# Delta attention: Gram matrices at the end of the projections, a sigmoid in quarters, state scalings moved, two heads ahead of the first spreading

## The reference

```python
q = silu(dwconv(x @ Wq)); k = silu(dwconv(x @ Wk)); v = silu(dwconv(x @ Wv))
a = sigmoid(x @ Wa + ba); beta = sigmoid(x @ Wb + bb)
for t in range(T):                       # per batch and head, S is 128 x 128
    err = S @ (k_t * D**-0.5) - v_t
    S = a_t * S - (beta_t * err) outer (k_t * D**-0.5)
    o_t = S @ q_t
out = (layernorm(o) * ln_g + ln_b) * sigmoid(x @ Wg) @ Wo
```

## Time and profile before

| what | value |
|---|---|
| median of 3 runs | 2659.15 us (2654.32 to 2659.25) |
| the profiled execution | 2658.91 us |
| its span | 2657.0 us |
| PE busy | 2083.4 us, 78% |
| DVE, ACT, POOL busy | 1521.6 (57%), 1182.6 (45%), 1037.5 (39%) |

### The profile page before, as it was taken

The page is one execution under the profiler, slowest core; times in us unless marked ns, Lnnn a source line. Parts: engine busy times, 40 slices in busy tenths (PEclk is TensorE's granted clock), DMA queues, the critical chain, the costliest instruction groups (busy, mean ns, idle before and its releaser), DMA issues. The chain is left out here.

```text
span 2657.0 us, 45220 instructions
## 1 busy us (share of the span) xinstructions
PE 2083.4 (78%) x16876; PEld 1611.6 (61%) x16888; DVE 1521.6 (57%) x3266; ACT 1182.6 (45%) x2893; POOL 1037.5 (39%) x965
## 2 busy tenths in 40 slices
PE   8497438978897987857798577977779676768798
PEld 5365225646565865746587466866668665546586
DVE  2222642237574344687676876767868678246532
ACT  3212411126364334754465545655456454326433
POOL 0222122210003552586335862467724757100254
PEclk9698769989998997958798687986689777889899
DMA  8422012110004212321222212322122222020430
GB/s 281 134 24 53 3 43 67 23 44 2 23 2 134 102 18 75 97 69 49 84 90 68 89 45 83 93 69 69 57 88 80 66 69 78 19 58 2 118 118 16
DMA packets 138317, 179.47 MB, mean 68 GB/s; under 512 B 62048, under 2 KB 114544, under 8 KB 132992
## 3 DMA queue, kind: packets, MB, share of 16 engines
q1 hardware_dynamic: 129952, 166.46, 20.5%
q0 software_dynamic: 8160, 10.26, 2.5%
HBM read 154.52 MB, written 22.17 MB: 66 GB/s over the span
## 5 line engine op out<-in xcount | busy, mean ns | idle before, releaser
L2672 DVE SCALAR_TENSOR_TENSOR XT<-M_delta,CW_delta,XT 128x256 f32<-128x256 f32 x576 | 250.0, 495 | 82.7 <-ACT M_delta L2463 52.6
L2146 PE MATMUL PS<-XP_delta,X 128*128 128x268 f32 (+1 forms) x1024 | 244.0, 391 | 15.5 <-DMA X<-in_L_attn_b_heads 15.5
L2146 PEld LDWEIGHTS PS<-XP_delta,X 128*128 128x128 f32 x1024 | 194.8, 191 | 68.2 <-DMA X<-in_L_attn_b_heads 19.3
L1541 PE MATMUL PS<-XP_rffn,UW_rffn 128*128 128x512 f32 x816 | 195.3, 396 | 5.1 <-POOL UW_rffn L1495 4.6
L1541 PEld LDWEIGHTS PS<-XP_rffn,UW_rffn 128*128 128x128 f32 x816 | 156.4, 192 | 38.9 <-issue 6.0
L1273 ACT ACTIVATE PR_attn<-PS,NM_attn 128x256 f32<-128x256 f32 (+1 forms) x384 | 131.0, 449 | 102.5 <-DVE NM_attn L1343 102.5
L1495 POOL TENSOR_TENSOR UW_rffn<-W_rffn,UW_rffn 128x512 fp32r<-128x512 f32 x34 | 43.7, 1286 | 298.8 <-ACT UW_rffn L1602 298.8
L561 POOL DMA_INDIRECT sums<-XS_moe,token_moe x46 | 71.7, 1559 | 220.8 <-ACT XS_moe L661 196.9
L2590 ACT ACTIVATE S_delta<-S_delta,AO_delta 128x128 f32<-128x128 f32 x512 | 156.9, 396 | 0.0
L1663 DVE TENSOR_TENSOR SU_rffn<-PS,CB_rffn 128x512 f32<-128x512 f32 x68 | 47.0, 692 | 179.7 <-PE PS L1541 157.3
L1504 POOL TENSOR_TENSOR HP_rffn<-HF_rffn,HP_rffn 128x512 fp32r<-128x512 f32 x68 | 92.5, 1380 | 116.3 <-ACT HP_rffn L1625 116.3
(11 more groups left out here) (459 smaller groups left out, 5271.4 us busy)
## 6 DMA issues: line engine op xcount, KB each, us to landing
M_delta<-gram_delta SPq DMA_DIRECT2D x32, 1280.0 KB, 5.9
X<-in_L_attn_b_heads SPq DMA_DIRECT2D x64, 512.0 KB, 3.5
EW<-in_L_ffn_w SPq DMA_DIRECT2D x24, 512.0 KB, 9.1
CB_rffn<-routes_rffn SPq DMA_DIRECT2D x20, 512.0 KB, 21.9
XN<-in_L_attn_b_outs SPq DMA_DIRECT2D x16, 512.0 KB, 3.6
F_delta<-in_L_attn_b_outs SPq DMA_DIRECT2D x4, 2048.0 KB, 9.5
W_rffn<-in_L_ffn_tiles SPq DMA_DIRECT2D x4, 1536.0 KB, 12.5
slots<-pad SPq DMA_DIRECT2D x2, 2967.0 KB, 14.3
```

The costliest lines, as they stand in the source:

```text
L1541: last = nc.tensor.matmul(PS[:, 4 + 2 * n + q, :], UW[qw][:, r, (q * KD + k) * P:(q * KD + k + 1) * P], XP[qx][:, k, n * NB:(n + 1) * NB], ...
L2146: last = nc.tensor.matmul(PS[:, 1 + i, 0:B * (WIN - halo)], WH[:, r, i, k, :], XP[:, k, :, n * BT + halo:n * BT + WIN], start=(k == 0), st ...
L2672: nc.vector.scalar_tensor_tensor(TMP[:, r, i], RAW[:, r, i, :, tau:tau + BT], CW[:, i, h, tau:tau + 1], TMP[:, r, i], ALU.mult, ALU.add).t ...
```

## The change

- Both halves' Gram matrices are made before the states phase, heads 0 to 13 first, then heads 14 and 15, which alone wait for the last silus and keys. `gram(1)` no longer follows the states. The order of DVE's four `gram_rows` and SP's count (3 instead of 2) follow this.
- The sigmoid over A is split into four of 1024 columns, one behind each of ACT's first four groups in the states phase of the first half; the fourth releases POOL.
- `cuts` go from 14, 14, 20, 16 scalings in chunks 0 to 3 to 18, 18, 24, 4. Those of chunk 3 stand before the key rows instead of between them.
- In a block after the first, PE's list has `head(n, 0)` before `spread(n - 1, 0)` and `head(n, 1)` right after `centre(n - 1, 1)`, ahead of the first two projects; ACT's list has `evacuate(n, 0)` before `square(n - 1, 1)`.

```diff
-                sp.wait_ge(gr_d, z["gr_d"] + 2)
+                sp.wait_ge(gr_d, z["gr_d"] + 3)
                 scatter(0, 0)
...
-            def gram(o):
-
-                for h in range(H):
+            def gram(o, first, last_h):
+
+                for h in range(first, last_h):
...
                     variance(n - 1, 0)
+                if n < NBLK:
+                    head(n, 0)
+                if n:
                     spread(n - 1, 0)
-                for k in range(1, H // 2 + 1):
+                    centre(n - 1, 1)
+                if n < NBLK:
+                    head(n, 1)
+                if n:
+                    variance(n - 1, 1)
+                    project(n - 1, 0)
+                    project(n - 1, 1)
+                    spread(n - 1, 1)
+                for k in range(2, H // 2 + 1):
...
                 pe.wait_ge(ev_d, z["ev_d"] + 3 * H)
-                pe.wait_ge(act_d, z["act_d"] + 3 * H)
                 pe.wait_ge(raw_d, z["raw_d"] + H)
-                pe.wait_ge(k_d, z["k_d"] + H)
-                gram(0)
+                for first, last in ((0, H - 2), (H - 2, H)):
+                    pe.wait_ge(act_d, z["act_d"] + 3 * last)
+                    pe.wait_ge(k_d, z["k_d"] + last)
+                    for o in range(NO):
+                        gram(o, first, last)
...
-                gram(1)
                 for o in range(NO):
                     key_products(n, o)
...
-                for k in range(1, H // 2 + 1):
+                if n < NBLK:
+                    evacuate(n, 0)
+                if n:
+                    square(n - 1, 1)
+                if n < NBLK:
+                    evacuate(n, 1)
+                    silus(n, 0)
+                for k in range(2, H // 2 + 1):
...
+                    if not o and g < 4:
+                        part = AF[:, g * BH * BT // 4:(g + 1) * BH * BT // 4]
+                        last = nc.scalar.activation(part, part, ACT.Sigmoid)
+                        if g == 3:
+                            last.then_inc(a_d, 1)
...
-            cuts = [0, 14, 28, 48, BH]
+            cuts = [0, 18, 36, 60, BH]
...
-                nc.scalar.activation(AF, AF, ACT.Sigmoid).then_inc(a_d, 1)
                 states(n, 0)
...
+                        if jj == NI - 1:
+                            decay_state(lane, last)
                         for r in rows[:2]:
                             key_rows(n, o, r)
...
-                        else:
+                        elif jj + 1 < NI:
                             decay_state(lane, last)
-                            if jj + 1 < NI:
-                                answer(n, ci)
+                            answer(n, ci)
...
-                dve.wait_ge(gr_mm, n * 4 + 2 * o + i + 1)
+                dve.wait_ge(gr_mm, n * 4 + 2 * i + o + 1)
...
-                gram_rows(n, 0, 0)
-                gram_rows(n, 0, 1)
+                for i in range(2):
+                    gram_rows(n, 0, i)
+                    gram_rows(n, 1, i)
                 for g in range(1, NS, 2):
                     state_copy(n, 0, g)
-                gram_rows(n, 1, 0)
-                gram_rows(n, 1, 1)
```

More of the change, by code:

```diff
@@ L2505, in heads_and_norm @@
                         evacuate(n, 2 * k - 2)
-                        if k > 1:
-                            silus(n, 2 * k - 3)
+                        silus(n, 2 * k - 3)
                         evacuate(n, 2 * k - 1)
```

## The result

The changed kernel takes 2634.41 us (median of 6 runs, 2631.31 to 2640.3) against 2659.13 for the kernel before in the same session (6 runs, 2654.32 to 2660.09): ratio 0.9912, 95% interval 0.9899 to 0.9925. The forecast was 2625, with a range of 2613 to 2639. So the kernel is 24.7 us faster where 34.2 were worked out.

A forecast was written before the change was run, and what follows sets the result against it. Waits at engine handovers (projections' end, last chunk, block border) were taken to bound the delta stage, PE the heads stage; 18.7 + 11.6 + 3.9 = 34.2 us off 2658.9 gave 2625 us, range 2613 to 2639.

The forecast's parts named there:

- Scalings moved, 18.7 forecast: Last chunk of each block: PE's turn of W starts 4.66 us sooner, four times, 18.7 us saved.
- the cap of 21.1: Last chunk: the turn cannot pay more than DVE's 5.27 us wait per block, 21.1 us in all.
- The cost in chunks 0 to 2: Four more scalings in each chunk add 1.2 us, taken to lie in ACT's idle time: no cost.
- a bound of 4.8: Second half's first chunk, scalings ahead of `answer`: lost cover costs at most 1.2 us a block, 4.8 in all.
- Gram matrices and quarters, 11.6 forecast: End of projections to DVE's `base`: 3.1 us sooner in three blocks, 2.3 in block 0, 11.6 in all.
- the row was right: Table load before the sigmoid: 1.30 us by the profile row, against the skill's 2.66 with drain.
- The rival of an ACT that falls behind in the quarters: States phase: ACT later by 1.28 us a block, 5.1 in all, paid through POOL; 2630 us, chance 0.05.
- Two heads ahead, 3.9 forecast: Three block borders: PE resumes 1.3 us sooner at each, 3.9 us saved, between -3 and 9.2.
- the cold stretch: Border: PE's first 3.5 us at clock 0.50 may stay the same (gain 1.3) or vanish (1.75 us more).
- half clock (28 ns passes): Rival: Gram passes before the states take 6.4 us, costing 2.9 us in three blocks; 2633 us, chance 0.12.
- no gain at the border: Rival: swapped heads give nothing, 2629 us, or 2632 with 1 us of new stall each; chance 0.07.

The follow-up runs named there:

- Experiments 4 and 8: 4: changed kernel with the old cuts in first halves only, 2624.08 us. 8: changed kernel with the last errors copied ahead of the scalings, 2623.59 us.
- experiment 7: Changed kernel with 32 instead of 16 idle PE transposes at the end of each first half; one execution, 2635.96 us.
- experiment 5: Changed kernel with the sigmoid whole again ahead of the states, Gram matrices staying at the end of the projections; 2639.97 us, ratio 0.992.
- experiment 10: Changed kernel with the last errors copied early, the sigmoid whole ahead of the states, and twelve idle PE transposes in the gap; 2616.06 us, ratio 0.9852.

## Why the prediction was right, and where its terms were off

The direction and the places were right. Two terms of the sum were mis-sized in the same direction, 7.3 us at the Gram matrices and quarters and 4.6 us in chunks 0 to 2; 2.3 us more than forecast at the turns and 1.2 more at the border made up for a part.

*Scalings moved, 18.7 forecast.* The turns gave 4.62 us a block, 18.5 in all, against the 4.66 worked out. The reading of the stall was right. A further 0.5, 1.6 and 0.4 us in blocks 0 to 2 came from the transposes of the turn, which now run at 1.00 instead of 0.50; the working had left them at their old length. That the 21.0 us in all stand just under the cap of 21.1 is chance: the cap was 5.27 us four times, read in block 0, and block 1 alone gave 6.2.

*The cost in chunks 0 to 2, forecast at nothing with a bound of 4.8.* It was 1.15 us a block, 4.6 of the 5.8 in the table's second row; the other 1.2 lie scattered over the chunks ahead and are not assigned. The bound was the right size, but it was put in the wrong place: the second half's first chunk, at `answer`, where the first gate still waited 1.07 us for PE afterwards, so it was covered. The cost fell in the first half's last chunk, where "the added 1.2 us lie in ACT's idle time" was false: ACT's queue there holds the error copies that release POOL. The step that failed is that I looked for who waits on ACT's gates and copies for PE, and not for the POOL product behind L2584. Experiments 4 and 8 show it from two sides.

*Gram matrices and quarters, 11.6 forecast.* 4.3 were measured. The parts: the passes ran at the full level, 15.6 ns against 15.8; POOL was last, as said; the table load took 1.28 us with the sigmoid 1.29 us behind its start, so the row was right. The drain that the Trainium skill adds (ScalarE: Activation LUTs, "What ACT_TABLE_LOAD costs") is not seen. In block 1 the release of POOL came 14.2 us behind head 15 where 13.3 were worked out, and `base` 18.8 us behind the release where 17.7 were: 0.9 + 1.1 = 2.0 us. The first is the fetch pause, less a margin that the working had by a misreading: the states started 6.05 us behind head 15 where 4.9 were worked out, and ACT's first copy followed them after 0.75 us where 1.1 were taken. The 1.15 us between the two in the earlier trace rows were no cost of PE: the old copy, at 1424.27, had been standing behind the sigmoid, which ended at 1424.33. The second is POOL's chain held up by DVE's key decays. The shortfall is 2.0, 2.0 and 1.7 us of the forecast 3.1 in blocks 1 to 3, and 1.6 of 2.3 in block 0, which has no fetch pause: there it is the same 1.1 us of POOL's chain and a release 16.5 us behind head 15 instead of 16.1. So the step that failed here is that the passes and POOL's chain were taken at the length that they have undisturbed. Neither mechanism stood among the rivals. The rival of an ACT that falls behind in the quarters, 1.3 us a block, came nearest in price, for a wrong reason: from its first copy to the release ACT took 7.4 us, as worked out (7.3).

The Trainium skill (Runtime: NRT & Kernel Launch, "Instruction fetch mechanics") has the fetch in blocks of 16 KiB, 256 instructions, and calls the cost of a crossing mostly hidden. The block size agrees with the trace; "mostly hidden" does not hold here, where 128 passes at 15.6 ns last 2.0 us and the engine then stood 1.2 to 1.4 us, up to 1.9 in experiment 7. On the other mechanism the Trainium skill (SBUF — State Buffer, "SBUF: two separate sides") says that DVE with two SBUF inputs and GpSimd take a shared port pair by an exclusive lock for the whole instruction. The trace agrees: 1.73 us for 0.61 on POOL, and 2.87 us for 0.41 on DVE, each ending just behind the other engine's instruction, 0.5 and 0.3 us after it.

*Two heads ahead, 3.9 forecast.* 5.1 in the profiles of the whole change, 2.9 in those of this part alone, 5.8 by its ratio; the forecast lies among them. The gains at the three borders, 1.0, 2.5 and 1.5 us, are the 1.2 to 1.3 us of waiting for the root, about as worked out, and what the cold stretch gained or lost in length: head 0 took 6.09, 5.50 and 5.51 us, 2.3, 1.7 and 1.8 over its full speed, where the same extra, spread over `spread(0)`, `centre(1)` and head 0, had been 2.3, 3.2 and 2.2 us before. So it neither stayed the same nor vanished; it lay between the two ends that were kept.

*The range.* 2634.4 lies inside 2613 to 2639, in part by luck. The range was made of the clock, the table load and the border, and none of these cost what had been kept for it; most of the 9.5 us went to the order on ACT in the first half, the fetch and POOL's chain, for which nothing had been kept there. The bound of 4.8 us for the cover was not among its parts. The rivals of half clock (28 ns passes) and of no gain at the border are refuted by the rows above.

*Left open.* What decides whether the clock falls after a short pause: 2.23 us of idle time in block 1 of experiment 5 left it at 1.00, 2.37 us in block 2 of the same execution and 2.18 us in block 1 of experiment 10 were followed by 0.50, for 17 and 3.4 us. A gap is not needed either: in block 3 of the changed kernel the clock fell at 2052 with no pause over 1.23 us behind head 15. The early copy together with the old cuts in the first half was not run; each alone brings the chunk to 14.0 to 14.2 us.

The scatter of the second half's last chunk goes with the clock. Here are the 3.5 us that begin 5 us into that chunk, in blocks 0 and 1 of the kernel before and block 2 of experiment 7; the chunks take 14.5, 13.2 and 15.6 us:

```profile
1286.65:1290.15 3.50, 3.50 (x13) 2.64 (x11) 3.26 (x9) 1.15 (x3) 0.00 (x0) 0.77 0.00 0
1605.89:1609.39 3.50, 2.75 (x13) 1.86 (x11) 3.02 (x8) 1.93 (x8) 0.00 (x0) 1.00 0.01 2
1919.88:1923.38 3.50, 3.50 (x10) 2.70 (x9) 3.23 (x10) 1.92 (x6) 0.00 (x0) 0.50 0.00 0
```

A low stretch begins ahead of this chunk in every block. Over the 48 blocks of the twelve kernels, the chunk takes 13.0 to 13.2 us where the clock is back at 1.00 within 5.0 us of the chunk's start, 14.2 to 15.1 where that takes 5.9 to 8.0 us, and 15.5 to 15.6 where it takes 8.5 or 8.6. What sets the end of the low stretch was not tested.

## What to carry to other kernels

An engine with idle time ahead of a wait is not free to take more work: ask for each thing it releases, on every engine, which is last. Here 1.2 us of ACT work beside a stall of PE was free for PE and cost 1.15 us by way of POOL, and putting the copy that releases POOL ahead of the scalings took it back (15.38 to 14.0 us a block).

When a serial stretch is shortened until small matmuls run back to back, price the instructions themselves: 256 of PE's are one fetch, and at 15.6 ns a pass they are used up faster than they come. And a long operation that delays PE's next work by 2 to 3 us can cost more through the clock than by its length; cutting it up, or giving PE twelve idle transposes, helped here: with the quarters the clock stayed at 1.00 in 17 of 24 blocks and with the transposes in three of four, against one of eight with the sigmoid whole and nothing in the gap.

## What the runs showed of the hardware that was not expected

- PE stands 1.0 to 2.2 us where pairs of weight load and 64-column matmul pass a boundary of 256 instructions at 15.6 ns a pass, with a 16384-byte transfer on the instruction queue (0.9 to 1.8 us) ahead of it. Moving the boundary by 16 pairs moved the stop by 16 passes. In the heads stage, where 16 matmuls last 3.76 us and 256 instructions therefore about 30 us, no such stop shows: PE is busy 77.85 of the 78.13 us from 1332.67 to 1410.80.
- DVE and POOL hold each other up for whole instructions: POOL 0.61 us to 1.73, DVE 0.41 us to 2.87, though each has its own list and no semaphore links them.
- With the sigmoid whole (3.62 us) PE's granted clock was 0.50 in the states for 7 to 17 us, in three of four blocks of one execution and in all four of another; with the quarters it was so for 3 to 10 us in 7 of the 24 blocks of six executions. A gap of 2.4 us can be followed by a loss several times as long: block 2 of experiment 5 took 38.5 - 30.4 = 8.1 us more than block 1.
